# Layer 3 of a routed-expert kernel: ScalarE instead of VectorE reads the up product

## The reference

```python
expert = jnp.argmax(opcode_onehot, axis=-1)
up = jnp.einsum('bsd,bhd->bsh', x, W_up[expert]) + b_up[expert][:, None, :]
gate = jnp.einsum('bsd,bhd->bsh', x, W_gate[expert]) + b_gate[expert][:, None, :]
hidden = jax.nn.silu(up) * gate
out = jnp.einsum('bsh,bdh->bsd', hidden, W_down[expert]) + b_down[expert][:, None, :]
x = x + out
```

## Time and profile before

| | us |
|---|---|
| median of 3 runs (lowest, highest) | 92.47 (92.28, 92.53) |
| the profiled execution | 92.08 |
| its span, first to last instruction | 90.3 |

### The profile page before, as it was taken

The page is one execution under the profiler, slowest core; times in us unless marked ns, Lnnn a source line. Parts: engine busy times, 40 slices in busy tenths (PEclk is TensorE's granted clock), DMA queues, the critical chain, the costliest instruction groups (busy, mean ns, idle before and its releaser), DMA issues.

```text
span 90.3 us, 1922 instructions
## 1 busy us (share of the span) xinstructions
PE 83.2 (92%) x620; PEld 77.3 (86%) x620; DVE 54.5 (60%) x123; ACT 28.0 (31%) x49; POOL 16.3 (18%) x19
## 2 busy tenths in 40 slices
PE   5999775999999799999999999999999999999950
PEld 5948673888887698999999999999999999999730
DVE  0249999899999533245465465465456547445770
ACT  2305580383727552202402402402302312211120
POOL 3246450046555970000000000000000000000000
PEclk9999999999999999999999999999999999999999
DMA  2994000769992000188489889988998888625001
GB/s 43 362 388 191 0 0 0 261 199 354 425 399 115 0 0 0 22 313 301 125 321 337 259 288 335 283 261 283 307 324 348 285 289 301 226 37 183 2 29 33
DMA packets 5768, 18.57 MB, mean 206 GB/s; under 512 B 640, under 2 KB 1920, under 8 KB 5760
## 3 DMA queue, kind: packets, MB, share of 16 engines
q1 hardware_dynamic: 5472, 18.16, 58.0%
q10 hardware_dynamic: 288, 0.32, 1.2%
HBM read 17.95 MB, written 0.52 MB: 205 GB/s over the span
## 4 chain that ended last, share of the span: by engine, by line
PE 63%; DVE 23%; DMA 5%; issue 4%; ACT 1%; ACTq 0%; DVEq 0%
PE bank L626 32%; PE bank L636 16%; PE bank L650 7%; DMA rest_sb<-in_rest 5%; DVE hid L442 5%; PE bank L666 4%; DVE p L345 2%; DVE wsel L423 1%; DVE p L353 1%; DVE val L362 1%; PE bank L597 1%; DVE eq L372 1%; DVE eq L361 1%; DVE hot L405 1%; PE bank L598 1%
## 5 line engine op out<-in xcount | busy, mean ns | idle before, releaser
L626 PE MATMUL bank<-x_t,pair_w 128*128 128x128 f32 (+1 forms) x256 | 31.3, 275 | 0.5 <-DVE hid L442 0.5
L626 PEld LDWEIGHTS bank<-x_t,pair_w 128*128 128x128 f32 x256 | 29.9, 192 | 0.8 <-issue 0.8
L444 DVE SCALAR_TENSOR_TENSOR hid<-gelu,wsel,bank 128x512 f32<-128x512 f32 x16 | 12.0, 748 | 21.8 <-PE bank L626 19.0
L279 ACT ACTIVATE gelu<-bank 128x512 f32<-128x512 f32 x24 | 14.1, 593 | 31.6 <-PE bank L626 27.6
L636 PE MATMUL bank<-hid,pair_w 128*128 128x128 f32 x128 | 16.9, 275 | 0.0
L636 PEld LDWEIGHTS bank<-hid,pair_w 128*128 128x128 f32 x128 | 15.7, 192 | 0.1
L247 POOL TENSOR_TENSOR hid_l<-hid,hid_h 128x512 fp32r<-128x512 f32 x8 | 10.2, 1286 | 10.1 <-ACT hid_h L298 10.1
L650 PE MATMUL bank<-x_t,w 128*128 128x128 f32 x64 | 8.7, 276 | 0.0
L650 PEld LDWEIGHTS bank<-x_t,w 128*128 128x128 f32 x64 | 7.9, 192 | 0.1
L285 ACT ACTIVATE tanh<-half 128x256 f32<-128x256 f32 (+1 forms) x9 | 3.5, 392 | 13.4 <-DVE half L473 13.4
L597 PE MATMUL bank<-x_h,shared_h 128*128 128x512 f32 x16 | 6.4, 399 | 1.1 <-DVE x_h L391 1.1
(11 more groups left out here) (67 smaller groups left out, 76.6 us busy)
## 6 DMA issues: line engine op xcount, KB each, us to landing
pair_w<-in_skill SPq DMA_DIRECT2D x16, 768.0 KB, 5.7
w<-in_layer SPq DMA_DIRECT2D x8, 384.0 KB, 5.4
shared_sb<-in_shared SPq DMA_DIRECT2D x3, 256.0 KB, 5.3
w_sb<-in_w SPq DMA_DIRECT2D x1, 576.0 KB, 4.5
x_t<-in_x SPq DMA_DIRECT2D x2, 256.0 KB, 4.0
out_x<-out_sb SPq DMA_DIRECT2D x8, 64.0 KB, 4.2
rest_sb<-in_rest ACTq DMA_DIRECT2D x1, 181.0 KB, 4.7
head_sb<-in_head ACTq DMA_DIRECT2D x1, 132.0 KB, 3.2
```

What stands on the lines that cost most here:

```text
L279: act.activation(gelu[:, n, :], ps[:, :], ACT.Gelu_apprx_tanh).then_inc(gelu_ready, 1)
L444: dve.scalar_tensor_tensor(hid[:, n, :], gelu[:, n, :], wsel[:, bass.DynSlice(weight, 1)], u_ps[n][:, :], ALU.mult, ALU.mult).then_inc(hid ...
L626: mm = pe.matmul(ps[:, S * t:S * (t + 1)], pair_w[:, slot, n, 128 * t:128 * (t + 1)], x2_t[:, columns(b)], start=True, stop=True)
```

## The change

1. The halved bias gets a tile of its own, `bhalf` [128, 2, 8], made by one more VectorE instruction at the end of `bias_columns`: a TENSOR_SCALAR from SBUF to SBUF over 16 elements per partition.
2. `halve3` and `tanh_step` go. `half_tanh3` on ScalarE reads the up product from PSUM twice per chunk: Identity with scale 0.5 and bias `bhalf` into half3, and Tanh with the same scale and bias into tanh3, so four ScalarE instructions of 128x128 per batch in place of one of 128x256 there and two of 128x128 on VectorE.
3. half3, tanh3, gate3 and hid3 exist twice and go by the parity of the batch. The waits that guard them look one batch further back.
4. TensorE's up and gate products tell of each chunk, with the waits in front of each chunk. In the last batch each of the four chunks has a bank of its own (banks 3, 2, 1, 4), and the up product waits for no reader of batch 6.
5. The last two batches on VectorE: `residual(7)` comes first, then `gated3(6)`, `silu_gate3(6)`, `gated3(7)`, `silu_gate3(7)` in two parts, `result(6)`, `result(7)`: `result(6)` stands behind the last batch's hidden values instead of ahead of them.

```diff
+        bhalf = sb("bhalf", [128, HC, B])
-        half3 = sb("half3", [128, HC, S])
+        half3 = sb("half3", [128, 2, HC, S])
...
-        def gate3_bank(b):
-            return bank[1] if is_last(b) else bank[5]
+        def up3_ps(b, c):
+            return (bank[3], bank[2])[c] if is_last(b) else bank[7]
+
+        def gate3_ps(b, c):
+            return (bank[1], bank[4])[c] if is_last(b) else bank[5]
...
-            def tanh_step(b, parts=1):
-                n = HC // parts
-                for c in range(parts):
-                    act.wait_ge(half3_ready, HC * b + n * (c + 1))
-                    act.activation(tanh3[:, n * c:n * (c + 1), :], half3[:, n * c:n * (c + 1), :],
-                                   ACT.Tanh).then_inc(tanh3_ready, 1)
+            def half_tanh3(b, q):
+
+                for c in range(HC):
+                    act.wait_ge(up3_done, HC * b + (c + 1 if is_last(b) else HC))
+                    if at_least(b, 2):
+                        act.wait_ge(gate3_ready, HC * (b - 1))
+                        act.wait_ge(hid3_ready, b - 1)
+                    ps, bias = up3_ps(b, c)[:, S * c:S * (c + 1)], bhalf[:, c, bass.DynSlice(b, 1)]
+                    act.activation(half3[:, q, c, :], ps, ACT.Identity, bias=bias, scale=0.5).then_inc(half3_ready, 1)
+                    act.activation(tanh3[:, q, c, :], ps, ACT.Tanh, bias=bias, scale=0.5).then_inc(tanh3_ready, 1)
...
                 then(dve.reduce_sum(bsel[:, :, :], bias_hot[:, :, :, :], axis=AX.X))
+                dve.tensor_scalar(bhalf[:, :, :], bsel[:, 0:HC, :], 0.5, None, ALU.mult).then_inc(bhalf_ready, 1)
...
-            def halve3(b):
-                dve.wait_ge(up3_done, b + 1)
-                if at_least(b, 1):
-                    dve.wait_ge(tanh3_ready, b)
-                for c in range(HC):
-                    dve.tensor_scalar(half3[:, c, :], up3_ps[:, S * c:S * (c + 1)], bsel[:, c, bass.DynSlice(b, 1)], 0.5,
-                                      ALU.add, ALU.mult).then_inc(half3_ready, 1)
...
+            def gated3(b, q, c):
+
+                dve.wait_ge(half3_ready, HC * b + c + 1)
+                dve.wait_ge(gate3_done, HC * b + (c + 1 if is_last(b) else HC))
...
-            halve3(B - 2)
             residual(B - 1, 1)
-            gated3(B - 2)
-            silu_gate3(B - 2)
-            halve3(B - 1)
-            gated3(B - 1)
+            for c in range(HC):
+                gated3(B - 2, 0, c)
+            silu_gate3(B - 2, 0)
+            for c in range(HC):
+                gated3(B - 1, 1, c)
+            silu_gate3(B - 1, 1, parts=HC)
             result(B - 2, 0)
-            silu_gate3(B - 1, parts=HC)
             result(B - 1, 1)
...
-            def product3(b, q, n):
+            def product3(b, q, n, c):
 
                 pe.wait_ge(w3_in[q], 16 * fills(b, q))
                 pe.wait_ge(x3_ready, b + 1)
                 if not at_least(b, 1):
                     pe.wait_ge(x2s_ready, 2)
-                elif n == 0 or not is_last(b):
-                    pe.wait_ge((half3_ready, gate3_ready)[n], HC * b)
-                ps, done = ((up3_ps, up3_done), (gate3_bank(b), gate3_done))[n]
+                elif not is_last(b):
+                    pe.wait_ge((tanh3_ready, gate3_ready)[n], HC * b)
+                ps, done = ((up3_ps(b, c), up3_done), (gate3_ps(b, c), gate3_done))[n]
+                pe.matmul(ps[:, S * c:S * (c + 1)], w3[:, q, n, 128 * c:128 * (c + 1)],
+                          x3_t[:, q, :], start=True, stop=True).then_inc(done, 1)
```

More of the change, by code:

```diff
@@ L103, in build @@
         x3_t = sb("x3_t", [C, 2, S])
-        half3 = sb("half3", [128, HC, S])
-        tanh3 = sb("tanh3", [128, HC, S])
-        gate3 = sb("gate3", [128, HC, S])
-        hid3 = sb("hid3", [128, HC, S])
+        bhalf = sb("bhalf", [128, HC, B])
+        half3 = sb("half3", [128, 2, HC, S])
+        tanh3 = sb("tanh3", [128, 2, HC, S])
+        gate3 = sb("gate3", [128, 2, HC, S])
+        hid3 = sb("hid3", [128, 2, HC, S])
         out_sb = sb("out_sb", [C, 2, S])
@@ L142, in build @@
         x3_ready = sem("x3_ready")
+        bhalf_ready = sem("bhalf_ready")
         up3_done, gate3_done, half3_ready, tanh3_ready, gate3_ready, hid3_ready = (
@@ L279, in gelu_step, with batch @@
                 act.activation(gelu[:, n, :], ps[:, :], ACT.Gelu_apprx_tanh).then_inc(gelu_ready, 1)
-            def tanh_step(b, parts=1):
-                n = HC // parts
-                for c in range(parts):
-                    act.wait_ge(half3_ready, HC * b + n * (c + 1))
-                    act.activation(tanh3[:, n * c:n * (c + 1), :], half3[:, n * c:n * (c + 1), :],
-                                   ACT.Tanh).then_inc(tanh3_ready, 1)
-            def batch(b, last=True):
+            def half_tanh3(b, q):
[7 more added lines that the diff above has]
+                    act.activation(tanh3[:, q, c, :], ps, ACT.Tanh, bias=bias, scale=0.5).then_inc(tanh3_ready, 1)
+            def batch(b, q, last=True):
                 gelu_step(NSH + TOP_K * b, 0, g_ps[0])
@@ L291, in batch @@
                 if last:
-                    tanh_step(b - 1)
+                    half_tanh3(b - 1, 1 - q)
             def round_hidden(k):
@@ L304, in _ @@
             round_hidden(NSH - 1)
-            batch(0, last=False)
-            batch(1)
+            batch(0, 0, last=False)
+            act.wait_ge(bhalf_ready, 1)
+            batch(1, 1)
             with act.Fori(1, B // 2) as j:
                 for q in range(2):
-                    batch(2 * j + q)
-            tanh_step(B - 1, parts=HC)
+                    batch(2 * j + q, q)
+            half_tanh3(B - 1, 1)
         @block.vector
@@ L476, in gated3 @@
[L476 to L488, removed]
+            def gated3(b, q, c):
+                dve.wait_ge(half3_ready, HC * b + c + 1)
+                dve.wait_ge(gate3_done, HC * b + (c + 1 if is_last(b) else HC))
+                dve.scalar_tensor_tensor(gate3[:, q, c, :], gate3_ps(b, c)[:, S * c:S * (c + 1)],
+                                         bsel[:, HC + c, bass.DynSlice(b, 1)], half3[:, q, c, :],
+                                         ALU.add, ALU.mult).then_inc(gate3_ready, 1)
@@ L489, in silu_gate3 @@
+            def silu_gate3(b, q, parts=1):
+                if at_least(b, 2):
+                    dve.wait_ge(out_done, b - 1)
                 n = HC // parts
                 for c in range(parts):
-                    dve.wait_ge(tanh3_ready, b + 1 + c)
-                    dve.scalar_tensor_tensor(hid3[:, n * c:n * (c + 1), :], tanh3[:, n * c:n * (c + 1), :], 1.0,
-                                             gate3[:, n * c:n * (c + 1), :], ALU.add, ALU.mult).then_inc(hid3_ready, 1)
+                    dve.wait_ge(gate3_ready, HC * b + n * (c + 1))
+                    dve.wait_ge(tanh3_ready, HC * b + n * (c + 1))
+                    dve.scalar_tensor_tensor(hid3[:, q, n * c:n * (c + 1), :], tanh3[:, q, n * c:n * (c + 1), :], 1.0,
+                                             gate3[:, q, n * c:n * (c + 1), :], ALU.add, ALU.mult).then_inc(hid3_ready, 1)
@@ L502, in batch @@
                 if last:
-                    halve3(b - 1)
-                    gated3(b - 1)
-                    silu_gate3(b - 1)
+                    for c in range(HC):
+                        gated3(b - 1, 1 - q, c)
+                    silu_gate3(b - 1, 1 - q)
             between = {0: lambda: stream2_rest(1), 1: softmax, 2: chosen_probabilities, 3: expert_weights, 4: bias_columns,
@@ L645, in product3, with both_chunks3 @@
                     pe.wait_ge(x2s_ready, 2)
-                elif n == 0 or not is_last(b):
-                    pe.wait_ge((half3_ready, gate3_ready)[n], HC * b)
-                ps, done = ((up3_ps, up3_done), (gate3_bank(b), gate3_done))[n]
-                for c in range(HC):
[L650 to L656, removed]
+                elif not is_last(b):
[3 more added lines that the diff above has]
+                          x3_t[:, q, :], start=True, stop=True).then_inc(done, 1)
+            def both_chunks3(b, q, n):
+                for c in range(HC):
+                    product3(b, q, n, c)
             def down3(b, q, parts=1):
@@ L665, in down3 @@
                         pe.wait_ge(hid3_ready, b + 1 + c * parts // HC)
-                    mm = pe.matmul(out_ps[:, 0:S], w3[:, q, 2, C * c:C * (c + 1)], hid3[:, c, :],
+                    mm = pe.matmul(out_ps[:, 0:S], w3[:, q, 2, C * c:C * (c + 1)], hid3[:, q, c, :],
                                    start=(c == 0), stop=(c == HC - 1))
@@ L677, in batch @@
                 if last:
-                    up_gate3(b - 1, 1 - q)
+                    both_chunks3(b - 1, 1 - q, 0)
+                    both_chunks3(b - 1, 1 - q, 1)
                 down(b, 0, q)
@@ L712, in _ @@
             down(B - 1, 0, 1)
-            product3(B - 2, 0, 0)
+            both_chunks3(B - 2, 0, 0)
             down(B - 1, 1, 1)
-            product3(B - 2, 0, 1)
```

(4 more changed lines are left out.)

1 line of the change is left out of this document (removed).

## The result

The changed kernel takes 93.16 us (median of 20 runs, 92.66 to 94.0), the kernel before 92.67 on the same chips (20 runs, 92.28 to 93.22). The ratio is 1.0046, with a 95% interval from 1.0025 to 1.0066: 0.43 us slower, between 0.23 and 0.61. The forecast was +0.23 with the halving of the bias held, and that is the case that came. On the 92.47 that the forecast started from, the ratio gives 92.9, inside its 91.5 to 93.1; the median of these runs is 0.06 above that range, because the kernel before came out 0.20 higher here as well. The profiled execution took 93.12, with a span of 91.0.

A forecast was written before the change was run, and what follows sets the result against it. TensorE, busy from about 30 to 84 us, was taken as the bound, so only changes ahead of 30.16 or behind 84 us count. 1.04 - 0.81 = +0.23 on the 92.47 median gave 92.7 us, range 91.5 to 93.1.

The forecast's parts named there:

- the held case: Beside GpSimd's subtraction, the new TENSOR_SCALAR waits until GpSimd lets go, costing 1.04 us; kernel 92.7 us, chance 0.57.
- The halved bias, +1.04: Between `bsel` and step 5's `hidden`, the new TENSOR_SCALAR delays VectorE and then TensorE: +0.08 to +1.04 us, +1.04 taken.
- The end, -0.81: In the last batches, `silu_gate3(7)` ends at 86.46 instead of 87.27 us and what follows keeps its length: -0.81 us.
- The middle, 0: In the middle batches TensorE stays full and ScalarE's four instructions finish before the next gelu needs it: 0 us.
- Not held: Rival: beside GpSimd the new one-tensor instruction runs unhindered, costing 0.08 us; kernel 91.74 us, chance 0.35.
- ScalarE as the end: Rival: in the last batch ScalarE's four instructions run late, the end 0.25 us later than before; 93.8 us, chance 0.05.
- Tables: Rival: Identity, Tanh and gelu share no ScalarE table, each switch costs 1.28 us, four in the last batch; 97.8, chance 0.03.

## Why the prediction was right, point by point

The sign of the sum was right, its size (+0.23) lies at the lower edge of what was measured (0.23 to 0.61), and both terms came from the right mechanism. Luck had a share in it. The choice of the held case had a chance of 0.57, and the chances of faster, same and slower were nearly even (0.34, 0.34, 0.32), so the sign by itself says little. The sum of the traces is as close as +0.22 to +0.23 only because the halving cost 0.10 less than forecast and a pause of 0.08 came in that was not in the sum. And the sum left out the 0.34 us outside the span.

- *The halved bias, +1.04.* Held, as taken; 0.94. The instruction ended where the step put it, 0.03 behind GpSimd. What was off is the next line, that step 5's `hidden` starts where the halving ends: it starts 0.08 before, as the instructions behind each other in the earlier trace rows do. The choice between held and not rested on the shape of the operands and on their all lying in SBUF; the runs confirm it (1.10 and 1.11 held, 0.17 without GpSimd, 0.17 as a reduction beside it). The rule of the Trainium skill named there (SBUF — State Buffer, Who interferes with whom) agrees with all of them, also with the writing GpSimd: 0.32 for an instruction of 0.17. That a `hidden` behind the one held by a memset isn't late is not in it.
- *The end, -0.81.* Measured -0.80, and ScalarE's instructions at 0.37 as taken, about 0.26 apart where 0.27 was. The estimate of 0.39 from the figures of the Trainium skill (ScalarE: Activation LUTs, What ACT_TABLE_LOAD costs) is 0.02 above the measured one. Two small misses on the way cancel: `silu_gate3(6)` starts 1.22 behind `residual(7)` where the step has 1.16, and `silu_gate3(7)` 0.55 behind `gated3(7)` where it has 0.61. The account of what the 0.81 is made of was wrong, though: `halve3(7)` gone for 0.64 and `result(6)` gone from in front for 0.26 reads as if each could be had alone. The total came from walking the new order step by step, and that was right; the split took durations out of the old order. The order alone brings 0.13, and all the rest without it 0.14.
- *The middle, 0.* TensorE full in both. The gelu behind ScalarE's new work waits for TensorE 1.15 us, more than the 0.87 before, as the step said. The pause of 0.08 was not in the sum.
- *The rivals.* Not held: refuted. ScalarE as the end: refuted, its last tanh ends 0.13 ahead of the last `gated3`. Tables: refuted, there are two loads in the changed kernel's trace, both ahead of the first gelu, as before.
- *What stays open.* The prediction took the time outside the span as unchanged (it added the +0.23 to the time and to the span alike). It grew by 0.34, and why is not shown. The traces' terms and this make 0.22 + 0.34 = +0.56, inside the measured 0.23 to 0.61 but above its middle; the mean spans by themselves, 91.01 against 90.95, differ by less than the +0.22 of the terms. The spans of a kernel's runs scatter by some 0.3 us, so the 0.1 to 0.2 us between these sums can't be told from noise. The short pauses of TensorE (0.08 in the changed kernel's trace, 0.31 in that of the reduction) differ from trace to trace; what brings them is open.

## What to carry to other kernels

Before a small instruction is added to VectorE, look at what GpSimd is doing at that very moment: an elementwise instruction whose tensors all lie in SBUF can last as long as GpSimd's, and sixteen elements (1.10 us) then take longer than the 512 of `hidden` (0.69). Routing work of no urgency belongs where VectorE waits anyway. And price a group of edits by walking the new order with the clock, not by adding up what each takes away: here two groups of edits worth 0.14 and 0.13 us were worth 0.80 together. Compare the runs' times with their spans as well: a change can add time that no row of the trace shows, here 0.34 us.

## What the runs showed of the hardware

- A VectorE TENSOR_SCALAR of 16 elements per partition, one input, float32, SBUF to SBUF: 0.17 us alone, 1.10 and 1.11 beside a GpSimd subtraction of 1.29 that began 0.22 earlier, 0.32 beside a GpSimd memset of 0.53 that began 0.23 earlier (one execution). A TENSOR_REDUCE of the same tiles beside the subtraction: 0.17.
- Behind the one held by the reading GpSimd the next VectorE instruction is 0.94 late; behind the one held by the memset it starts 0.11 after the held one's start, and is not late (one execution).
- ScalarE reads 128 float32 columns from PSUM with a bias column and writes SBUF in 0.37 us, and four such follow each other 0.25 to 0.27 apart, Identity and Tanh in turn, with no table load between them.
